# Attention and routing on one core: routing in the next slot, and weights split while the first batch runs

## The chip, the cores and the metric

The kernel runs on one core of one Trainium2 chip. The metric is the device time of a run in microseconds. The profile is of one execution, and its time is given beside that of the timed runs below.

## What is computed

64 batches of 128 tokens of width 512, all fp32. Each batch attends to its own context of 128 tokens, and then each token goes to two of twelve small experts:

```python
q = rms_norm((layernorm(x) @ Wq) by 16 heads of 128) * q_norm_w
k = rms_norm((ctx @ Wk) by 4 heads) * k_norm_w;  v = ctx @ Wv      # 4 query heads share one k, v
x = x + softmax(q @ k.T / sqrt(128)) @ v @ Wo
h = layernorm(x);  logits = h @ gate_w.T                            # 12 experts, the best 2 of each token
x = x + sum over the 2 of  weight * (silu((h @ w1.T) * (h @ w3.T)) @ w2.T)
# an expert takes at most ceil(8192 * 1.25 / 12) tokens per choice list, in token order
```

## The kernel before

The work has three stages: a load of the weights, a loop over the 64 batches (attention and routing), and the experts (`experts`, which the diff leaves alone). A fp32 product is made of three passes of TensorE over a high and a low part of each factor (`PARTS`: hi hi, hi lo, lo hi). So each operand is split: ScalarE writes the high part as a copy in a shorter format, VectorE (POOL for x and the context) writes the low part as the difference.

**Weights.** 40 lots of 256 KB (4 of Wk, 4 of Wv, 16 of Wq, 16 of Wo) go through six staging buffers. Per lot: SyncE (SP) loads it; ScalarE makes the high part (L927); VectorE makes the low part (L1182). A Wq lot is centred first: TensorE computes the column means (`mean`, L706) and VectorE subtracts them (L1178). All of it stands before the loop in each engine's program, and so do the scaling of the norm weights (`scale_weights`), the split of the gate (`split_gate`), and two fills (`d_sent`): the lists of experts in DRAM and 1.8 MB of x copied behind the output. POOL waits for both fills ahead of its loop.

**The loop.** Every engine runs `body(b)` with the same four slots g = 0 to 3, one for each group of four heads; the order in which calls stand there is the order in which the engine works, in order, and semaphores join the engines. A slot holds steps of several batches at once. With u = 4b + g:

- PE: scores of u (L760); half of the keys or values of batch b+1, and queries of u+3 (L716); out projection of u-2 (L787); attend of u-1 (L775). In slot 1 also `route(b-2)` (L796, L797), which writes the logits into OT_B, attend's bank; in slot 3 `positions(b-2)`.
- The probabilities: VectorE takes the maxima (L1031) and nmax (L1034); ScalarE the exponentials (L890) from PSUM; VectorE the reciprocal (L1040) and the normalisation (L1043); ScalarE the high part (L898); VectorE the low part (`split_p`, L1049). SP then turns both (a DMA transpose, `turn_p`), and in the next slot ScalarE (`widen_p`, L904) and VectorE (L1056) bring them to fp32 for attend. In ScalarE's program `widen_p` of u-1 stands ahead of the exponentials of u.
- Between these stand the other steps: the query split (L880, L1022); the key norm (`norm_k`, L997) and key split (`split_k`, L865 and L1003), then `turn_k`, for which the scores of slot 0 wait; `residual` (L1065), `stats_2` (L1069), `norm2` (L1078) of batch b-1; `copy_logits` (L1088), `choose` (L1094 to L1103), `place` of the routing; `split_xn2` and `turn_xn2`, for which `route` waits.

VectorE's order in slots 2 and 3 before, from its `body`:

```python
# slot 1, end: ..., split_p, split_q, sum_k(b+1), choose(b-2)
# slot 2: residual(b-1), maxima, split_o, widen_p, norm_k(b+1), normalise, sum_q, split_p, split_q, stats_2(b-1), split_k(b+1)
# slot 3: maxima, split_o, widen_p, norm2(b-1), normalise, count(b-2), sum_q, split_p, split_q
```

`kn`, into which `norm_k` writes, is the buffer from which `route` reads the turned x, so `norm_k` waits for `lg_done`. The body runs as straight code for b = -1 to 2 and 62 to 66 and as a hardware loop between.

Of the kernel before, what the change touches and what calls it, by code (L numbers as in the profile page):

```python
# [399 lines left out]
def build(nc, x, xT, cT, wq, wk, wv, wo, qw, kw, gateT, w13, w2T, out):  # L400
# [42 lines left out]
    with keep:  # L443
# [13 lines left out]
        with ExitStack() as ctx:  # L457
# [4 lines left out]
            wqp = [sb(f"wq_{p}", [128, NC, NH * HD], f32r) for p in ("hi", "lo")]  # L462
            wkvp = [sb(f"wkv_{p}", [128, 2, NC, NG * HD], f32r) for p in ("hi", "lo")]
            wop = [sb(f"wo_{p}", [128, NH, HID], f32r) for p in ("hi", "lo")]
# [52 lines left out]
            def heads(bank):  # L517
                return bank[:, :].rearrange("p (h t) -> p h t", h=HPG)

            STAGES = (0, 1, 5, 9, 10, 11)  # L520
            NST = len(STAGES)
            d_w = [sem(f"d_w_stage{i}") for i in range(NST)]
            d_small, d_c, d_x, d_xs, d_xr = sem("d_small"), sem("d_c"), sem("d_x"), sem("d_xs"), sem("d_xr")
# [30 lines left out]
            LOTS = ([("k", n) for n in range(NG)] + [("v", n) for n in range(NG)] + [("q", n) for n in range(NH)]  # L554
                    + [("o", n) for n in range(NH)])
            NLOT = len(LOTS)
            V_IN, Q_IN = 2 * NG, 2 * NG

            def stage(l):
                flat = work[:, STAGES[l % NST], :]  # L560
                return flat if LOTS[l][0] == "o" else flat.rearrange("p (c n) -> p c n", c=NC)

            def lot_parts(l):

                kind, n = LOTS[l]
                cols = slice(n * 128, (n + 1) * 128)
                if kind in "kv":
                    return [w[:, "kv".index(kind), :, cols] for w in wkvp]
                if kind == "q":
                    return [w[:, :, cols] for w in wqp]  # L570
                return [w[:, n, :] for w in wop]

            def lot_landed(eng, l):
                eng.wait_ge(d_w[l % NST], 16 * (l // NST + 1))

            def mean_cols(n):

                return (S_B, OT_B, WO_B, SQ_B)[n % 4][:, 0:128]
# [12 lines left out]
            def _(sp):  # L591
# [50 lines left out]
                for l, (kind, n) in enumerate(LOTS):  # L642
                    if l == NG:
                        load_c(0)
                    if l == V_IN:
                        sp.dma_start(gate[:, :, :], gateT).then_inc(d_small, 16)
                        sp.dma_start(wb[:, :], qw.broadcast_to([128, HD])).then_inc(d_small, 16)
                        sp.dma_start(work[:, 6, 0:HD], kw.broadcast_to([128, HD])).then_inc(d_small, 16)
                        load_x(0)
                    if l == Q_IN + NG:  # L650
                        load_stat(0)
                    if l >= NST:
                        sp.wait_ge(w_lo, l - NST + 1)
                    cols = slice(n * 128, (n + 1) * 128)
                    src = (wo[cols, :] if kind == "o" else wq_v[:, :, cols] if kind == "q"
                           else wkv_v["kv".index(kind)][:, :, cols])
                    sp.dma_start(stage(l), src).then_inc(d_w[l % NST], 16)
                sp.wait_ge(s_const, 1)
                sp.dma_start(table_d[LIST1:, :].rearrange("(e p t) o -> p e (t o)", p=128, t=NT),
                             sentinel[:, :, :].rearrange("p t o -> p (t o)")[:, None, :].broadcast_to(  # L660
                                 [128, E, 2 * NT])).then_inc(d_sent, 16)


                sp.dma_start(out[T:T + CP, :], x.rearrange("b t n -> (b t) n")[0:CP, :]).then_inc(d_sent, 16)
                sp.wait_ge(w_lo, NLOT)
                sp.wait_ge(wqk_done, 1)

                def body(b):
                    for g in range(NG):
# [18 lines left out]
                        if g == 0 and live(b - 2):  # L688
                            turn_xn2(b - 2)

# [7 lines left out]
            def _(pe):  # L698

                pe.wait_ge(s_mw, 1)  # L700
                def mean(n):
                    l = Q_IN + n
                    lot_landed(pe, l)
                    wait(pe, w_cent, n - 3)
                    for c in range(NC):
                        mm = nc.tensor.matmul(mean_cols(n), mean_w[:, :], stage(l)[:, c, :],  # L706
                                              start=(c == 0), stop=(c == NC - 1))
                    mm.then_inc(w_mean, 1)
# [11 lines left out]
                def weights_in(b, n):  # L720

                    if isinstance(b, int) and b == 0:
                        pe.wait_ge(w_lo, n)
# [3 lines left out]
                def keys(b, half):  # L727
                    if half == 0:
                        weights_in(b, NG)
                        wait(pe, c_lo, b + 1)  # L730
                        wait(pe, k_nrm, b)
# [4 lines left out]
                def values(b, half):  # L736
                    if half == 0:
                        weights_in(b, V_IN)
                        wait(pe, v_lo, b)
# [4 lines left out]
                def queries(b, g):  # L744
                    u = 4 * b + g
                    weights_in(b, Q_IN + HPG * (g + 1))
# [32 lines left out]
                def out_project(b, g):  # L779
                    u = 4 * b + g  # L780
                    wait(pe, ot_lo, u + 1)
                    if g == 0:
                        wait(pe, x1_done, b)
                    for h in range(HPG):
                        weights_in(b, Q_IN + NH + HPG * g + h + 1)
# [6 lines left out]
                def route(b):  # L792
                    wait(pe, d_xT, 16 * (b + 1))
                    wait(pe, ot_lo, min(4 * b + 8, NU) if isinstance(b, int) else 4 * b + 8)
# [14 lines left out]
                for n in range(NH):  # L809
                    mean(n)  # L810
                pe.wait_ge(s_const, 1)

                def body(b):
                    for g in range(NG):
                        cur, far = (b, g), off(b, g, 3)
                        before, last = off(b, g, -1), off(b, g, -2)
                        if live(b):
                            scores(*cur)
# [6 lines left out]
                        if g == 1 and live(b - 2):  # L825
# [12 lines left out]
            def _(act):  # L838
# [83 lines left out]
                for l, (kind, n) in enumerate(LOTS):  # L922
                    if kind == "q":
                        act.wait_ge(w_cent, n + 1)
                    else:
                        lot_landed(act, l)
                    nc.scalar.copy(lot_parts(l)[0], stage(l)).then_inc(w_hi, 1)  # L927
                    if l == V_IN - 1:
                        split_c(0)
                act.wait_ge(wqk_done, 1)  # L930

                def body(b):
                    for g in range(NG):
                        cur, near, far = (b, g), off(b, g, 2), off(b, g, 3)
                        before, last = off(b, g, -1), off(b, g, -2)
                        if live(last[0]):
# [7 lines left out]
                        if g == 2 and live(b - 2):  # L944
                            exp_diff(b - 2)
# [14 lines left out]
                        if g == 2 and live(b + 1):  # L960
                            split_k(b + 1)
# [5 lines left out]
            def _(dve):  # L967
# [179 lines left out]
                def split_gate():  # L1147

                    for k in range(3):
# [8 lines left out]
                def scale_weights():  # L1158

# [14 lines left out]
                for l in range(NLOT):  # L1174
                    if l + 1 < NLOT and LOTS[l + 1][0] == "q":
                        n, part = LOTS[l + 1][1], stage(l + 1)
                        dve.wait_ge(w_mean, n + 1)
                        nc.vector.tensor_tensor(part, part, mean_cols(n)[:, None, :].broadcast_to([128, NC, 128]),  # L1178
# [192 lines left out]
```

## Time and profile before

| | us |
|---|---|
| timed runs, median (lowest, highest) | 2662.54 (2662.12, 2664.76) |
| the profiled execution | 2652.94 |
| its span | 2651.2 |
| weights before the loop's first step on VectorE | 0 to 55 |
| first and last slot-0 scores (batches 0 and 63) | 79.33 and 2277.68 |
| experts and what comes before them | 2278 to 2651 |

(2277.68 - 79.33) / 63 = 34.89 us for one batch. "Rows" below are lines of the profile: a row of the timeline has start and duration in us, engine, line of the code, operation, output and input, and in brackets how long the engine was idle before it and what ended that. The duration of an instruction includes a tail that overlaps the next: L1003 is 0.66 us long and the next row starts 0.58 us after it. Costs are taken from start to start where both rows are there.

### The profile page before, as it was taken

Reading aid. Unit: us, or ns where it says so; the run is one execution under the profiler, and the core shown is the slowest. Engines: PE = TensorE matmul, PEld = TensorE weight load, DVE = VectorE, ACT = ScalarE, POOL = GpSimd, SP = SyncE. Lnnn points to the kernel's source line nnn. Section 1 sums busy time; section 2 is a strip of 40 time slices with the busy share of each in tenths; the row PEclk is TensorE's granted clock in tenths of the full one; section 3 lists DMA queues with packets and bytes.
Section 4 is the critical chain, followed back from the end, with each engine's and each line's share of the span. In section 5 each row is a group of like instructions: output and inputs, shape, how many; then the busy total and the mean of one; then the engine's idle time right before and its main releaser. Section 6 shows DMA issues by size and latency. Waiting matters only on the chain. (4 is left out here: it accounts for less than half of the span.)

```text
span 2651.2 us, 51686 instructions
## 1 busy us (share of the span) xinstructions
PE 2422.2 (91%) x12985; PEld 1875.8 (71%) x12985; DVE 2082.9 (79%) x5478; ACT 1646.5 (62%) x4789; POOL 1112.9 (42%) x1279
## 2 busy tenths in 40 slices
PE   3899999999999999999999999999999999749883
PEld 3777777777777777777777777777777777525451
DVE  5688888888888888888888888888888878737552
ACT  4566766666666666666666666666666666515441
POOL 0334334343433443434333344344343434258885
PEclk8999999999999999999999999999999999969875
DMA  7455555555555555555555555555555545449997
GB/s 214 84 118 118 122 125 119 125 117 120 127 118 118 116 119 127 119 123 120 118 127 120 120 115 117 126 121 121 123 118 124 123 105 113 97 116 189 182 180 98
DMA packets 778098, 331.20 MB, mean 125 GB/s; under 512 B 695340, under 2 KB 707884, under 8 KB 778032
## 3 DMA queue, kind: packets, MB, share of 16 engines
q1 hardware_dynamic: 754960, 287.61, 48.8%
q0 software_dynamic: 22912, 43.16, 9.1%
q8 instruction: 13, 0.21, 0.0%
q14 instruction: 21, 0.17, 0.0%
q10 hardware_dynamic: 192, 0.04, 0.0%
HBM read 108.15 MB, written 57.71 MB: 63 GB/s over the span
## 5 line engine op out<-in xcount | busy, mean ns | idle before, releaser
L904 ACT CAST pt_hi<-work 128x512 fp32r<-128x512 f16 x256 | 158.9, 621 | 617.9 <-DMA work<-work 617.9
L890 ACT ACTIVATE work<-pb,small 128x128 f32<-128x128 f32 x1024 | 454.5, 454 | 27.4 <-DVE small L1034 27.4
L716 PE MATMUL pb<-wq_hi,x_hi 128*128 128x512 f32 x1024 | 408.8, 399 | 32.2 <-POOL x_lo L1265 22.4
L787 PE MATMUL pb<-wo_hi,ot_hi 128*128 128x512 f32 x1024 | 413.7, 404 | 3.2 <-DVE ot_lo L970 3.0
L716 PE MATMUL pb<-wq_lo,x_hi 128*128 128x512 f32 x1024 | 401.4, 392 | 0.0
L716 PE MATMUL pb<-wq_hi,x_lo 128*128 128x512 f32 x1024 | 401.1, 392 | 0.0
L787 PE MATMUL pb<-wo_lo,ot_hi 128*128 128x512 f32 x1024 | 401.0, 392 | 0.0
L787 PE MATMUL pb<-wo_hi,ot_lo 128*128 128x512 f32 x1024 | 400.4, 391 | 0.0
L1288 POOL TENSOR_TENSOR small<-small 128x4 f32<-128x4 f32 x256 | 155.8, 609 | 544.7 <-DVE small L1016 544.7
L1022 DVE SCALAR_TENSOR_TENSOR work<-pb,small,work 128x128 f16<-128x128 f32 x1024 | 286.7, 340 | 45.1 <-ACT work L880 45.1
L880 ACT ACTIVATE work<-pb,small 128x128 f16<-128x128 f32 x1024 | 291.3, 366 | 0.0
L1291 POOL TENSOR_TENSOR small<-small 128x4 f32<-128x4 f32 x256 | 267.4, 1044 | 29.5 <-POOL small L1288 18.7
L1049 DVE TENSOR_TENSOR work<-work 128x512 f16<-128x512 f32 x256 | 251.3, 982 | 18.1 <-ACT work L898 12.0
L1265 POOL TENSOR_TENSOR x_lo<-work,x_hi 128x512 fp32r<-128x512 f32 x64 | 82.3, 1286 | 424.6 <-ACT x_hi L849 378.4
L716 PEld LDWEIGHTS pb<-wq_hi,x_hi 128*128 128x128 f32 x1024 | 193.6, 189 | 94.0 <-issue 29.0
L787 PEld LDWEIGHTS pb<-wo_hi,ot_hi 128*128 128x128 f32 x1024 | 192.9, 188 | 47.7 <-DVE ot_lo L970 10.7
L716 PEld LDWEIGHTS pb<-wq_hi,x_lo 128*128 128x128 f32 x1024 | 194.0, 189 | 41.4
L716 PE MATMUL pb<-wkv_hi,c_hi 128*128 128x512 f32 x512 | 222.7, 435 | 0.1
L787 PEld LDWEIGHTS pb<-wo_hi,ot_lo 128*128 128x128 f32 x1024 | 193.2, 189 | 41.5
L716 PEld LDWEIGHTS pb<-wq_lo,x_hi 128*128 128x128 f32 x1024 | 194.1, 190 | 39.2
L760 PEld LDWEIGHTS pb<-work 128*128 128x128 f16 x3072 | 172.3, 98 | 68.8 <-issue 68.8
L787 PEld LDWEIGHTS pb<-wo_lo,ot_hi 128*128 128x128 f32 x1024 | 193.6, 189 | 33.9
(144 smaller groups left out, 5297.6 us busy)
## 6 DMA issues: line engine op xcount, KB each, us to landing
work<-x SPq DMA_DIRECT2D x128, 256.0 KB, 3.2
work<-cT SPq DMA_DIRECT2D x64, 256.0 KB, 2.8
work<-xT SPq DMA_DIRECT2D x64, 256.0 KB, 3.2
out<-work SPq DMA_DIRECT2D x64, 256.0 KB, 4.7
xn_scratch<-work SPq DMA_DIRECT2D x64, 256.0 KB, 2.0
work<-work SPq DMA_TRANSPOSE x640, 3.3
work<-wq SPq DMA_DIRECT2D x16, 256.0 KB, 3.1
work<-wo SPq DMA_DIRECT2D x16, 256.0 KB, 3.5
```

What stands on the lines that cost most here:

```text
L716: mm = nc.tensor.matmul(bank[:, :], lhs[a][:, c, :], rhs[b_][:, c, :], start=(c == 0 and n == 0), stop=(c == NC - 1 and n == 2))
L760: mm = nc.tensor.matmul(S_B[:, h * 128:(h + 1) * 128], qT16[:, 4 * a + h, :], kT16[:, 4 * b_ + g, :], start=(n == 0), stop=(n == 2))
L787: mm = nc.tensor.matmul(WO_B[:, :], otp[a][:, h, :], wop[b_][:, g * HPG + h, :], start=(g == 0 and h == 0 and n == 0), stop=(g == NG - 1 a ...
L880: hi = nc.scalar.activation(q16[:, h, :], Q_BS[g % 2][:, h * 128:(h + 1) * 128], ACT.Copy, scale=q_rms[g % 2][:, h:h + 1])
L890: ex = nc.scalar.activation(probs[:, cols], S_B[:, cols], ACT.Exp, bias=nmax[:, h:h + 1], scale=esc, accum_out=psums[:, h:h + 1])
L904: nc.scalar.copy(ptp[0][:, :, :], pT16[:, HI, :]).then_inc(pt_hi, 1)
L1022: lo = nc.vector.scalar_tensor_tensor(out=q16[:, 4 + h, :], in0=Q_BS[g % 2][:, h * 128:(h + 1) * 128], scalar=q_rms[g % 2][:, h:h + 1], in ...
L1049: nc.vector.tensor_tensor(p16[:, LO, :], probs.rearrange("p (h t) -> p h t", h=HPG), p16[:, HI, :], ALU.subtract).then_inc(p_lo, 1)
L1265: nc.gpsimd.tensor_tensor(xp[1][:, :, :], raw_x.rearrange(by_chunk, c=NC), xp[0][:, :, :].bitcast(f32), ALU.subtract).then_inc(x_lo, 1)
L1288: nc.gpsimd.tensor_tensor(q_ms, q_ssq, eps_x.broadcast_to([128, HPG]), ALU.add).then_inc(q_m, 1)
L1291: nc.gpsimd.tensor_tensor(q_rms[g % 2], q_ms, neghalf, ALU.pow).then_inc(q_r, 1)
```

## The change

Two parts. **Routing:** `route` moves from slot 1 to slot 2 on TensorE, `copy_logits` and `choose` with it on VectorE, attend's wait for the copied logits from g = 0 to g = 1. Around it `norm_k` goes from ahead of `normalise` to behind `split_q` in slot 2, `split_k` from the end of slot 2 to slot 3 ahead of the exponentials (ScalarE) and of `norm2` (VectorE), `exp_diff` from slot 2 to the end of slot 3. **Weights:** the raw weights are loaded in ten lots of 1 MB into the space of the low parts, where VectorE replaces them in place; the steps of a lot stand inside `body` at the slots in `FEED`. SP issues the lots of k, q, v; ScalarE those of Wo, in slots 0 and 1 of batch 0. The gate is split in slot 0 of batch 1, the fills are issued in slot 1 of batch 1, and POOL waits for them in batch 2. An instruction still covers 128 x 512 elements: four per lot.

```diff
+            W_SHAPES = (("wq", [128, NC, NH * HD]), ("wkv", [128, 2, NC, NG * HD]), ("wo", [128, NH, HID]))
+            with ExitStack() as before:
+                wq_raw, wkv_raw, wo_raw = (before.enter_context(nc.sbuf_tensor(f"{n}_raw", shape, f32))
+                                           for n, shape in W_SHAPES)
+            wq_lo, wkv_lo, wo_lo = (sb(f"{n}_lo", shape, f32r) for n, shape in W_SHAPES)
...
+            LOTS = [("k", 0), ("q", 0), ("v", 0), ("q", 1), ("q", 2), ("q", 3)] + [("o", n) for n in range(NG)]
+            FEED = {(-1, 0): (0,), (-1, 1): (1,), (-1, 2): (2, 3), (-1, 3): (4,), (0, 0): (5,),
+                    (0, 2): (6,), (0, 3): (7,), (1, 0): (8,), (1, 1): (9,)}
...
@@ sync
+                load_c(0)
+                load_lot(0)
+                load_x(0)
...
+                for l in range(1, 6):
+                    load_lot(l)
...
+                        if g == 1 and isinstance(b, int) and b == 1:
+                            fill_tables()
@@ tensor
+                def mean(l):
+                    n = LOTS[l][1]
+                    pe.wait_ge(d_w[l], 16)
+                    wait(pe, w_cent, NC * (n - 1))
                     for c in range(NC):
+                        mm = nc.tensor.matmul(mean_bank(n)[:, :], mean_w[:, :], raw(l)[:, c, :],
                                               start=(c == 0), stop=(c == NC - 1))
...
@@ attend
                     if g == 0:
                         wait(pe, v_lo, b + 1)
+                    if g == 1:
                         wait(pe, lg_cp, b - 1)
@@ tensor, body
+                        for l in lots(b, g):
+                            if LOTS[l][0] == "q":
+                                mean(l)
                         if live(b):
                             scores(*cur)
...
-                        if g == 1 and live(b - 2):
+                        if g == 2 and live(b - 2):
                             route(b - 2)
@@ scalar
+                def head_of_lot(l):
+                    kind, n = LOTS[l]
+                    if kind != "q":
+                        act.wait_ge(d_w[l], 16)
+                    for c in range(NC):
+                        if kind == "q":
+                            act.wait_ge(w_cent, NC * n + c + 1)
+                        nc.scalar.copy(lot_parts(l)[0][:, c, :], raw(l)[:, c, :]).then_inc(w_hi, 1)
...
+                        for l in lots(b, g):
+                            head_of_lot(l)
+                        if g < 2 and isinstance(b, int) and b == 0:
+                            load_wo(6 + 2 * g)
+                            load_wo(7 + 2 * g)
...
-                        if g == 2 and live(b - 2):
-                            exp_diff(b - 2)
+                        if g == 3 and live(b + 1):
+                            split_k(b + 1)
                         if live(b):
                             exps(*cur)
...
-                        if g == 2 and live(b + 1):
-                            split_k(b + 1)
+                        if g == 3 and live(b - 2):
+                            exp_diff(b - 2)
@@ vector
+                def rest_of_lot(l):
+                    kind, n = LOTS[l]
+                    hi, lo = lot_parts(l)
+                    if kind == "q":
                         dve.wait_ge(w_mean, n + 1)
+                        for c in range(NC):
+                            nc.vector.tensor_tensor(raw(l)[:, c, :], raw(l)[:, c, :], mean_bank(n)[:, :],
+                                                    ALU.subtract).then_inc(w_cent, 1)
+                    for c in range(NC):
+                        dve.wait_ge(w_hi, NC * l + c + 1)
+                        nc.vector.tensor_tensor(lo[:, c, :], raw(l)[:, c, :], hi[:, c, :].bitcast(f32),
+                                                ALU.subtract).then_inc(w_lo, 1)
...
+                        if g == 1 and isinstance(b, int) and b == -1:
+                            scale_weights()
+                            dve.wait_ge(wqk_done, 6)
+                        for l in lots(b, g):
+                            rest_of_lot(l)
+                        if g == 0 and isinstance(b, int) and b == 1:
+                            split_gate()
...
-                        if g == 2 and live(b + 1):
-                            norm_k(b + 1)
+                        if g == 3 and live(b + 1):
+                            split_k(b + 1)
                         if g == 3 and live(b - 1):
                             norm2(b - 1)
                         if live(b):
                             normalise(*cur)
-                        if g == 1 and live(b - 2):
+                        if g == 2 and live(b - 2):
                             copy_logits(b - 2)
...
+                        if g == 2 and live(b + 1):
+                            norm_k(b + 1)
-                        if g == 1 and live(b - 2):
+                        if g == 2 and live(b - 2):
                             choose(b - 2)
                         if g == 2 and live(b - 1):
                             stats_2(b - 1)
-                        if g == 2 and live(b + 1):
-                            split_k(b + 1)
@@ gpsimd
-                pool.wait_ge(d_sent, 32)
...
+                        if g == 1 and isinstance(b, int) and b == 2:
+                            pool.wait_ge(d_sent, 32)
```

## Rows read from the trace of the kernel before

**Rows 1.** Waits, 400 to 1900 us, 43 batches: who waited for whom, total us, times, longest.
```profile
ACT pt_hi L904 <- DMA work<-work: 415.3, 172, 3.1
...
DVE small L1040 <- ACT work L890: 101.5, 129, 1.1
...
PE pb L796 <- DMA work<-work: 41.0, 43, 1.1
```

**Rows 2.** The page: engines, and DMA issues with KB each and us to landing.
```profile
PE 2422.2 (91%) x12985; PEld 1875.8 (71%) x12985; DVE 2082.9 (79%) x5478; ACT 1646.5 (62%) x4789; POOL 1112.9 (42%) x1279
...
work<-work SPq DMA_TRANSPOSE x640, 3.3
```

**Rows 3.** Timeline, VectorE, L1049 of batch 0 and of one steady batch: start us, us.
```profile
87.90 1.35 DVE L1049 TENSOR_TENSOR work<-work 128x512 f16<-128x512 f32 x1 [0.35 <-ACT work L898]
...
97.08 0.69 DVE L1049 TENSOR_TENSOR work<-work 128x512 f16<-128x512 f32 x1
...
105.13 0.69 DVE L1049 TENSOR_TENSOR work<-work 128x512 f16<-128x512 f32 x1
...
1018.08 1.31 DVE L1049 TENSOR_TENSOR work<-work 128x512 f16<-128x512 f32 x1
...
1027.16 1.23 DVE L1049 TENSOR_TENSOR work<-work 128x512 f16<-128x512 f32 x1 [0.16 <-ACT work L898]
...
1036.14 0.69 DVE L1049 TENSOR_TENSOR work<-work 128x512 f16<-128x512 f32 x1
...
1044.84 0.69 DVE L1049 TENSOR_TENSOR work<-work 128x512 f16<-128x512 f32 x1
...
1052.92 1.31 DVE L1049 TENSOR_TENSOR work<-work 128x512 f16<-128x512 f32 x1
```

**Rows 4.** Timeline, VectorE, end of slot 1 to slot 3 of the steady batch.
```profile
1038.83 0.16 DVE L1094 MAX8 small<-small 128x8 f32<-128x12 f32 x1
...
1039.67 0.68 DVE L1065 TENSOR_TENSOR work<-work,pb 128x512 f32<-128x512 f32 x1
...
1040.99 0.23 DVE L1034 TENSOR_SCALAR small<-small 128x4 f32<-128x4 f32 x1
...
1042.22 1.13 DVE L997 SCALAR_TENSOR_TENSOR work<-pb,small,wqk_rows 128x128 f32<-128x128 f32 x4
...
1046.93 0.68 DVE L1069 BATCH_NORM_STATS2 small<-work 128x6 f32<-128x512 f32 x1
...
1047.80 0.66 DVE L1003 TENSOR_TENSOR work<-work 128x512 f16<-128x512 f32 x1
1048.38 0.69 DVE L1031 TENSOR_REDUCE small<-pb 128x4 f32<-128x512 f32 x1
...
1051.33 0.18 DVE L1040 RECIPROCAL small<-small 128x4 f32<-128x4 f32 x1 [0.62 <-ACT work L890]
```

**Rows 5.** Timeline, ScalarE, slots 2 and 3 of the steady batch.
```profile
1040.10 0.62 ACT L904 CAST pt_hi<-work 128x512 fp32r<-128x512 f16 x1 [1.94 <-DMA work<-work]
...
1041.26 0.46 ACT L890 ACTIVATE work<-pb,small 128x128 f32<-128x128 f32 x1 [0.43 <-DVE small L1034]
...
1045.73 0.64 ACT L865 CAST work<-work 128x512 f16<-128x512 f32 x1
...
1048.90 0.62 ACT L904 CAST pt_hi<-work 128x512 fp32r<-128x512 f16 x1 [2.05 <-DMA work<-work]
1049.43 0.46 ACT L890 ACTIVATE work<-pb,small 128x128 f32<-128x128 f32 x1
```

**Rows 6.** Groups by line, 0 to 60 us: xcount, busy us, mean ns, idle before.
```profile
L706 PE MATMUL pb<-work,mean_w 128*128 128x128 f32 x128 | 18.3, 299 | 18.8 <-DMA work<-wq 18.7
...
L1182 DVE TENSOR_TENSOR wq_lo<-work,wq_hi 128x512 fp32r<-128x512 f32 x16 | 11.0, 685 | 0.1
```

**Rows 7.** Busy time by stretch: us, busy and count of each engine, clock, DMA share, GB/s.
```profile
0.00:33.00 33.00, 15.46 (x107) 14.07 (x108) 19.32 (x36) 13.79 (x22) 2.86 (x14) 1.00 0.74 210
```

**Rows 8.** DMA issues of the whole span: xcount, KB each, median us to landing.
```profile
out<-x SPq DMA_DIRECT2D x1, 1792.0 KB, 11.7
```

More of the change, by code:

```diff
@@ L518, in heads @@
                 return bank[:, :].rearrange("p (h t) -> p h t", h=HPG)
[L520 to L523, printed above, removed]
+            d_w = [sem(f"d_w_lot{i}") for i in range(2 + 2 * NG)]
+            d_small, d_gate, d_c, d_x, d_xs, d_xr = sem("d_small"), sem("d_gate"), sem("d_c"), sem("d_x"), sem("d_xs"), sem("d_xr")
             d_x1, d_xn2, d_sent = sem("d_x1_stored"), sem("d_xn2_stored"), sem("d_sentinel")
@@ L551, in build, with lots, lot_of, raw @@
             block = ctx.enter_context(nc.Block())
[L554 to L561, printed above, removed]
-            def lot_parts(l):
[L565 to L578, printed above, removed]
+            LOTS = [("k", 0), ("q", 0), ("v", 0), ("q", 1), ("q", 2), ("q", 3)] + [("o", n) for n in range(NG)]
+            FEED = {(-1, 0): (0,), (-1, 1): (1,), (-1, 2): (2, 3), (-1, 3): (4,), (0, 0): (5,),
+                    (0, 2): (6,), (0, 3): (7,), (1, 0): (8,), (1, 1): (9,)}
+            def lots(b, g):
+                return FEED.get((b, g), ()) if isinstance(b, int) else ()
+            def lot_of(l, wq_, wkv_, wo_):
+                kind, n = LOTS[l]
+                if kind in "kv":
+                    return wkv_[:, "kv".index(kind), :, :]
+                if kind == "q":
+                    return wq_[:, :, n * 512:(n + 1) * 512]
+                return wo_[:, n * HPG:(n + 1) * HPG, :]
+            def lot_parts(l):
+                return lot_of(l, wq_hi, wkv_hi, wo_hi), lot_of(l, wq_lo, wkv_lo, wo_lo)
+            def raw(l):
+                return lot_of(l, wq_raw, wkv_raw, wo_raw)
+            def mean_bank(n):
+                return (OT_B, WO_B)[n % 2]
+            def chunks_done(kind, n=0):
+                return NC * (LOTS.index((kind, n)) + 1)
             def loop(eng, body):
@@ new lines, in fill_tables @@
+                def fill_tables():
+                    sp.dma_start(table_d[LIST1:, :].rearrange("(e p t) o -> p e (t o)", p=128, t=NT),
+                                 sentinel[:, :, :].rearrange("p t o -> p (t o)")[:, None, :].broadcast_to(
+                                     [128, E, 2 * NT])).then_inc(d_sent, 16)
+                    sp.dma_start(out[T:T + CP, :],
+                                 x.rearrange("b t n -> (b t) n")[0:CP, :]).then_inc(d_sent, 16)
+                load_c(0)
@@ L793, in route @@
                     wait(pe, d_xT, 16 * (b + 1))
-                    wait(pe, ot_lo, min(4 * b + 8, NU) if isinstance(b, int) else 4 * b + 8)
+                    wait(pe, ot_lo, min(4 * b + 9, NU) if isinstance(b, int) else 4 * b + 9)
                     for c in range(NC):
```

84 lines of the change are left out of this document (26 added, 58 removed).

## Prediction

> **What bounds the kernel now.** I read the page first: TensorE is busy 91% of the span, more than any other engine [rows 2]. Then the waits of 43 steady batches [rows 1]. TensorE has one row there: `route` (L796) waits for a transposed tile, 41.0 us in 43 times, 0.95 us a batch. That looks like the bound and its one gap. But the same table has no row in which VectorE or SP waits for TensorE. ScalarE waits for the turned probabilities in every slot (415.3 us, 172 times = 4 x 43) and VectorE waits for ScalarE's exponentials (101.5 us). So there is a second loop, beside TensorE: `split_p` (L1049), DMA, `widen_p` (L904), exponentials (L890), reciprocal (L1040), normalise, `split_p` of the next slot.
>
> Third view: the timeline of one steady batch. The five starts of L1049 [rows 3] give the four slots: 9.08 (into slot 0), 8.98 (slot 1), 8.70 (slot 2), 8.08 (slot 3), sum 34.84 us, which is the pitch of the whole loop, (2277.68 - 79.33)/63 = 34.89. Slot 3 is to be followed link by link: L1049 at 1044.84; L904 at 1048.90, 4.06 later, as soon as the DMA lands; first exponential 0.53 later, 1049.43; L1040 at 1051.33, 1.90 later, freed by the exponentials (0.62 idle before it); L1049 1.59 later, 1052.92 [rows 3 to 5]. There is no slack in it. This loop, through ScalarE, VectorE and the DMA, makes the pitch; TensorE runs ahead of it and takes its spare time at `route`, whose tile is turned behind `turn_p` on the same queue.
>
> **Routing, slot 2.** `choose` leaves the end of slot 1: 0.84 us from L1094 to L1065 [rows 4]. Now the exponentials start at 1041.26 after 0.43 us of waiting for nmax [rows 5]; nmax is done at 1040.99 + 0.23 = 1041.22 [rows 4], so then at 40.38. ScalarE is ready at 1040.10 + 0.53 = 40.63, `exp_diff` being gone from that place. They start at 40.63. `norm_k` no longer stands before the reciprocal, so the two links of slot 3 follow: 40.63 + 1.90 + 1.59 = 44.12 instead of 44.84: **-0.72**. A control for this: batch 0 had no `choose` and no `exp_diff`, and its slot 2 took 105.13 - 97.08 = 8.05 [rows 3], against 8.70, a saving of 0.65. `copy_logits` ahead of `split_p` waits for `route`; TensorE is done with it before (its queries of that slot are needed by ScalarE's square, right behind the exponentials), and the 0.1 us reduction fits beside ScalarE's L898: 0, at worst 0.2.
>
> **Routing, slot 3.** Count from L1049 of slot 2. `split_q` ends at 46.93 - 44.84 = 2.09 (start of L1069). Before: `stats_2` 0.87, `split_k` 0.58, then maxima at 3.54 [rows 4], and nmax came just in time for ScalarE. After: `norm_k` 1.05 (1.13 less the 0.08 that overlaps), `choose` 0.84, `stats_2` 0.87, maxima at 4.85. From maxima to exponentials: 41.26 - (39.67 + 0.60 of the residual) = 0.99. So the exponentials start at 5.84; ScalarE's own path, 4.06 + 0.53 + 0.53 for `split_k` that now stands there (L865), would allow 5.12 [rows 5] and is hidden under it. Reciprocal at 7.74: VectorE, with `split_k` now between, is free at 4.85 + (51.33 - 48.38 - 0.62) + 0.58 = 7.76, the same. L1049 at 7.76 + 1.59 = 9.35 instead of 8.08: **+1.27**. The bounds: if the two delays didn't add and only the reordered `split_k` counted, +0.53 (ScalarE alone); if the transposes crowd each other, +1.6: `turn_k` is now issued some 2 us ahead of `turn_p`, and a transpose takes 3.3 us to land [rows 2], so up to 0.3 may be added.
>
> **Routing, slots 0 and 1, and TensorE.** ScalarE's and VectorE's orders are as before, so 9.08 and 8.98 stay. `turn_k` goes out behind `split_k` at 4.85 + 0.99 - 0.1 + 0.9 (the output and probability splits) + 0.58 = 7.2 to 7.8, lands at about 11, and slot 0's scores can start then; they take under 1 us. Maxima of slot 0 stand at 9.35 + 1.31 + 1.1 = 11.8 and nmax is wanted only 4.06 + 0.5 + 0.5 after L1049: hidden by 2 us. TensorE has 33.9 us of work a batch in 34.84 and the stall at `route` goes; it waits elsewhere (the key tile, the output split), and frees nobody. **The sum of the loop is -0.72 + 1.27 = +0.55 us a batch**, times 62 batches with routing: +34 us; bounds +0.3 to +0.9 a batch, +19 to +56.
>
> **Weights.** I follow the chain to `split_p` of slot 0, batch 0, which stood at 87.90 [rows 3]. A centring pass or low part takes 0.60 start to start (0.685 long [rows 6]), so a q lot costs VectorE 8 x 0.60 = 4.8 us, others 2.4. The mean of a whole q lot is 4 times the columns of an old one: at most 18.3/4 = 4.6 us [rows 6], less if weight loads carried part of it; I take 3.5. DMA moved 210 GB/s in the first 33 us [rows 7]: the context, k, x, small ones and q0 are 3.0 MB, 14.3 us, landed at 15. Then in series, because queries(0,g) waits for its lot, the mean of the next lot stands behind them on TensorE, and VectorE waits for that mean: mean 18.5; q0 split 23.5; queries 27.5 (slow clock); mean q1 31; v and q1 split 36; queries 39; mean q2 42.5; split 47.3; queries 50.3; mean q3 53.8 (scores of slot 0 behind it); split 58.6; queries(0,3) 61.5; square, sum, `split_p` 64. That is 24 us earlier than 87.90; VectorE's work alone (44 passes of 0.60 and the rest) sets a floor near 45, a slower clock and 4.6 us means put it at 70: gain 18 to 40.
>
> What it gives back inside batches 0 and 1: four Wo lots, 2.4 us each on VectorE ahead of the maxima; batch 0's slots have some 0.9 to 1.9 us of slack there, so 1.5, 1.9, 0.5, 1.3. ScalarE's heads lie in its wait for the DMA. `split_gate` 1.1. 4 MB of Wo move on another queue beside the transposes (20 us at 210 GB/s): 3 us of later landings. The fill, 11.7 us alone [rows 8], stands in SP's queue ahead of slot 2's `turn_p`, which comes 8.7 us later: 3 us, at most 11.7. Together 12 (5 to 25). The net of the start is 24 - 12: **-12 us** (+5 to -30). The experts and the drain are untouched.
>
> On whose share of DMA time the 3 us hang: the Trainium skill, page "DMA: Bandwidth & Descriptors", section "Queues, rings and completion order", has each DMA engine take turns by packet between the rows of queues that have work. No row of the kernel before shows ScalarE loads beside transposes; by that rule alone a transpose of 3.3 us beside them would double, 3.3 us for each of the two or three slots, and the sum would be 4 to 7 us higher.
>
> **Sum.** 2652.94 (span and 1.7 us around it) + 34 - 12 = 2675. The timed median stands 9.6 us above the profiled execution; the difference carries over: 2662.5 + 22 = **2684.5**.
>
> **Rivals.**
> - *A: TensorE is the bound.* The stall at `route` goes and nothing replaces it: 62 x 0.95 = -59, start -12: 2591. For it: 91% busy, one gap with one cause. Against: nobody waits for TensorE, and the loop of the probabilities has no idle link. It would also need that loop to lose over 1 us a batch where the edits add to it. Chance 0.07. [...]
> - *B: slot 3 costs no more than slot 2 saves.* With the lower bound, +0.53 - 0.72, or both parts of `choose` and `norm_k` finding gaps: loop 0 to -0.2, start -12: 2645 to 2650. Against: rows 4 are back to back. Chance 0.17.
> - *C: the key tile decides (slower side).* `turn_k` lands at 11; if scores of slot 0 come over 2 us later than I have it, maxima, nmax and exponentials wait for TensorE, and each us beyond is paid 62 times: at 1 us more, 2684.5 + 62 = 2746. Chance 0.10.
> - *D: the loop as forecast, but the start gains 30 net*: 2666. Inside my range. Chance 0.08; the forecast itself 0.58.
>
> The forecast's own range is 2660 to 2707. The range of 8 in 10 takes B in and leaves A and C out: 2646 to 2712. A measurement here tells about 0.2% (5.3 us) from no change. Faster by more: A, nearly all of B, a little of the forecast: 0.26. Within: 0.12. Slower: 0.62.
>
> **What would show it.** In the new trace: slots of L1049 of about 9.1, 9.0, 8.0, 9.35; first exponential of slot 3 released by nmax, not by ScalarE's order; no TensorE wait at L796's successor, but one of about 1 us at the scores of slot 0 for the key tile, and short ones at the out projection for `ot_lo`; pitch 35.4; `split_p` of batch 0, slot 0, near 64. I am wrong if slot 3 stays under 8.7, or if the pitch falls towards 33.9.

## The result and the profile after

The changed kernel takes 2702.45 us in the median of 4 runs (2701.61 to 2703.17), the kernel before 2662.33: ratio 1.0151, 95% interval 1.0133 to 1.0168, 40.1 us slower. The forecast was 2684.5, 22 us slower.

The view that decides is the timeline of VectorE over one steady batch, as in [rows 3, 4]: start us, us, engine, line. Line numbers have moved: L1077 is `split_p` (L1049 before), L1025 `norm_k` (L997), L1122 `choose` (L1094), L1097 `stats_2` (L1069), L1059 the maxima (L1031), L1068 the reciprocal (L1040).

```profile
1498.85 1.31 DVE L1077 TENSOR_TENSOR work<-work 128x512 f16<-128x512 f32 x1
...
1507.96 1.24 DVE L1077 TENSOR_TENSOR work<-work 128x512 f16<-128x512 f32 x1 [0.16 <-ACT work L912]
...
1517.03 0.69 DVE L1077 TENSOR_TENSOR work<-work 128x512 f16<-128x512 f32 x1
...
1525.06 0.69 DVE L1077 TENSOR_TENSOR work<-work 128x512 f16<-128x512 f32 x1
...
1527.14 1.12 DVE L1025 SCALAR_TENSOR_TENSOR work<-pb,small,wqk_rows 128x128 f32<-128x128 f32 x4
1528.18 0.17 DVE L1122 MAX8 small<-small 128x8 f32<-128x12 f32 x1
...
1529.03 0.69 DVE L1097 BATCH_NORM_STATS2 small<-work 128x6 f32<-128x512 f32 x1
...
1529.90 0.69 DVE L1059 TENSOR_REDUCE small<-pb 128x4 f32<-128x512 f32 x1
...
1532.80 0.18 DVE L1068 RECIPROCAL small<-small 128x4 f32<-128x4 f32 x1
...
1534.39 1.32 DVE L1077 TENSOR_TENSOR work<-work 128x512 f16<-128x512 f32 x1
```

The starts of L1077 give the slots: 1498.85 to 1507.96 (slot 0, 9.11), to 1517.03 (slot 1, 9.07), to 1525.06 (slot 2, 8.03), to 1534.39 (slot 3, 9.33), together 35.54 where the kernel before had 34.84 [rows 3]. In slot 3 `norm_k`, `choose`, `stats_2` and the maxima follow each other with no gap: `norm_k` at 2.08 after L1077, `choose` at 3.12, `stats_2` at 3.97, maxima at 4.84, reciprocal at 7.74, L1077 at 9.33. ScalarE in slots 2 and 3 shows the same from its side (L918 is `widen_p`, L879 `split_k`, L904 the exponentials):

```profile
1521.02 0.62 ACT L918 CAST pt_hi<-work 128x512 fp32r<-128x512 f16 x1 [1.98 <-DMA work<-work]
1521.56 0.46 ACT L904 ACTIVATE work<-pb,small 128x128 f32<-128x128 f32 x1
...
1529.17 0.62 ACT L918 CAST pt_hi<-work 128x512 fp32r<-128x512 f16 x1 [2.44 <-DMA work<-work]
1529.70 0.61 ACT L879 CAST work<-work 128x512 f16<-128x512 f32 x1
1530.89 0.46 ACT L904 ACTIVATE work<-pb,small 128x128 f32<-128x128 f32 x1 [0.58 <-DVE small L1062]
```

In slot 2 the exponentials follow `widen_p` at once; the 0.43 us of waiting of [rows 5] is gone. In slot 3 they now wait 0.58 us for nmax; `split_k`, which stands ahead of them, is done before that and costs nothing here. The waits from 400 to 1900 us, 42 batches (who waited for whom, total, times, longest):

```profile
ACT pt_hi L918 <- DMA work<-work: 435.5, 169, 3.1
...
ACT work L904 <- DVE small L1062: 29.7, 42, 1.0
...
PE pb L818 <- DVE ot_lo L998: 22.9, 42, 0.7
PE pb L800 <- DVE ot_lo L998: 20.8, 42, 0.5
...
PE pb L772 <- DMA work<-work: 13.5, 42, 0.4
```

TensorE no longer waits at `route`. It waits at `positions` (L818) and the out projection (L800) for the output split and at the scores (L772) for the key tile, 57.2 us in 42 batches, 1.36 us each, against 0.95 us before [rows 1]. So it got 0.4 us more of waiting where a wait was taken from it.

Means of the slots, worked out from the starts of `split_p` in 12 batches of each trace up to 700 us:

| kernel | slot 0 | 1 | 2 | 3 | pitch |
|---|---|---|---|---|---|
| before | 9.07 | 9.02 | 8.71 | 8.04 | 34.84 |
| after | 9.11 | 9.04 | 8.05 | 9.33 | 35.53 |

**The start.** `split_p` of batch 0, slot 0, is at 69.72 us instead of 87.90 [rows 3]: 18.2 us earlier. At slot 0 of batch 2 it stands at 157.89 instead of 156.10: all given back, and 1.8 more. One trace fixes such a difference only to a us or two: in the seven traces with the old load of the weights the first `split_p` comes at 86.39 to 88.66, and in the five of them whose batches 0 and 1 run as before that of slot (2,0) comes at 154.48 to 156.10. The slots of batches 0 and 1 one by one, from (0,1) to (2,0): 14.84, 9.57, 10.01, 10.17, 10.00, 7.99, 14.73, 10.86, where the kernel before has 9.18, 8.05, 8.05, 8.65, 9.08, 8.03, 8.02, 9.14. Two are long. ScalarE's row in slot (0,1), with its DMA issues (ACTq):

```profile
62.59 1.03 ACTq L949 DMA_DIRECT2D wo_raw<-wo  x2
...
68.87 0.37 ACTq L949 DMA_DIRECT2D wo_raw<-wo  x1
...
80.07 0.62 ACT L918 CAST pt_hi<-work 128x512 fp32r<-128x512 f16 x1 [9.33 <-DMA work<-work]
```

The transpose that SP issued at 71.15 releases `widen_p` at 80.07, 8.9 us later (the median on the page of this profile is 3.2), while the four Wo lots of 1 MB that ScalarE issued from 62.59 to 69.28 are landing. That issue and those of slot (1,3) on SP, then ScalarE in slot (1,3):

```profile
71.15 1.24 SPq L640 DMA_TRANSPOSE work<-work  x1
...
126.98 0.77 SPq L663 DMA_DIRECT2D out<-x  x1
127.86 1.53 SPq L635 DMA_TRANSPOSE work<-work  x1
```

```profile
138.40 1.14 ACT L894 ACTIVATE work<-pb,small 128x128 f16<-128x128 f32 x4 [6.14 <-DMA work<-work]
...
139.88 0.65 ACT L918 CAST pt_hi<-work 128x512 fp32r<-128x512 f16 x1
```

L663 is the fill of the output, 1.8 MB. Right behind it on SP stands `turn_q` (L635), issued at 127.86; it releases ScalarE's split of the queries (L894) at 138.40, 10.5 us later, after 6.14 us idle. `widen_p` and VectorE's `split_q` stand behind that.

**The account.** The last `split_p` is 41.1 us later than before (2351.32, 2310.24), the first step of the experts (`first_n`) 39.0 later. The rest of the span, unchanged code, took 319.3 us in the profiled execution and 308.0 in that of before; in the other profiles it is 315 to 320 on the chip where the kernel before took 2660.9 (315.2 with the loop of the kernel before, in e8 below) and 309 to 312 elsewhere (312.4 with the changed loop, in e2). So 11.3 of the 50.3 us between the two spans go with the execution, not with the change. The timed medians, 40.1 apart, agree with the 39.0.

### The profile page after: what moved, and what is told of

Same layout as the page of the kernel before. It is cut to its first block and busy times, and to the rows that moved or that the text cites. A ratio compares the mean times of both kernels' runs of the same rounds, so it can differ in the third digit from the quotient of the medians.

```text
span 2701.5 us, 51516 instructions
## 1 busy us (share of the span) xinstructions
PE 2455.9 (91%) x12889; PEld 1878.1 (70%) x12889; DVE 2079.6 (77%) x5478; ACT 1646.6 (61%) x4789; POOL 1107.4 (41%) x1279
## 5 line engine op out<-in xcount | busy, mean ns | idle before, releaser
L918 ACT CAST pt_hi<-work 128x512 fp32r<-128x512 f16 x256 | 159.0, 621 | 655.7 <-DMA work<-work 655.7
L904 ACT ACTIVATE work<-pb,small 128x128 f32<-128x128 f32 x1024 | 454.5, 454 | 51.1 <-DVE small L1062 51.1
L800 PE MATMUL pb<-wo_hi,ot_hi 128*128 128x512 f32 x1024 | 420.1, 410 | 41.2 <-DVE ot_lo L998 41.2
L728 PE MATMUL pb<-wq_hi,x_hi 128*128 128x512 f32 x1024 | 403.2, 394 | 18.9 <-DVE wq_lo L1216 13.6
L800 PE MATMUL pb<-wo_lo,ot_hi 128*128 128x512 f32 x1024 | 401.5, 392 | 0.0
L800 PE MATMUL pb<-wo_hi,ot_lo 128*128 128x512 f32 x1024 | 401.3, 392 | 0.0
L1326 POOL TENSOR_TENSOR small<-small 128x4 f32<-128x4 f32 x256 | 171.0, 668 | 530.5 <-DVE small L1044 530.5
L1050 DVE SCALAR_TENSOR_TENSOR work<-pb,small,work 128x128 f16<-128x128 f32 x1024 | 286.8, 341 | 53.4 <-ACT work L894 53.4
L894 ACT ACTIVATE work<-pb,small 128x128 f16<-128x128 f32 x1024 | 291.3, 366 | 6.5 <-DMA work<-work 6.5
L1329 POOL TENSOR_TENSOR small<-small 128x4 f32<-128x4 f32 x256 | 258.7, 1011 | 29.5 <-POOL small L1326 18.7
L800 PEld LDWEIGHTS pb<-wo_hi,ot_hi 128*128 128x128 f32 x1024 | 193.0, 189 | 103.5 <-DVE ot_lo L998 69.3
L1077 DVE TENSOR_TENSOR work<-work 128x512 f16<-128x512 f32 x256 | 250.6, 979 | 17.7 <-ACT work L912 11.7
L772 PEld LDWEIGHTS pb<-work 128*128 128x128 f16 x3072 | 173.4, 98 | 102.4 <-issue 53.2
L772 PE MATMUL pb<-work 128*128 128x128 f16 x3072 | 217.2, 221 | 25.0 <-DMA work<-work 24.0
L800 PEld LDWEIGHTS pb<-wo_hi,ot_lo 128*128 128x128 f32 x1024 | 193.4, 189 | 42.8
```

Source lines behind the costliest of these rows:

```text
L728: mm = nc.tensor.matmul(bank[:, :], lhs[a][:, c, :], rhs[b_][:, c, :], start=(c == 0 and n == 0), stop=(c == NC - 1 and n == 2))
L772: mm = nc.tensor.matmul(S_B[:, h * 128:(h + 1) * 128], qT16[:, 4 * a + h, :], kT16[:, 4 * b_ + g, :], start=(n == 0), stop=(n == 2))
L800: mm = nc.tensor.matmul(WO_B[:, :], otp[a][:, h, :], wop[b_][:, g * HPG + h, :], start=(g == 0 and h == 0 and n == 0), stop=(g == NG - 1 a ...
L894: hi = nc.scalar.activation(q16[:, h, :], Q_BS[g % 2][:, h * 128:(h + 1) * 128], ACT.Copy, scale=q_rms[g % 2][:, h:h + 1])
L904: ex = nc.scalar.activation(probs[:, cols], S_B[:, cols], ACT.Exp, bias=nmax[:, h:h + 1], scale=esc, accum_out=psums[:, h:h + 1])
L918: nc.scalar.copy(ptp[0][:, :, :], pT16[:, HI, :]).then_inc(pt_hi, 1)
```

## Experiments

Each was timed beside the kernel before on the same chip; its median there was 2652.3 for e1, e2, e3 and e7, 2660.9 for e4, e5, e6 and e8, and 2656.0 for e9 to e12. Slots and pitches come from the timelines as above.

**Half and half.** `e1_weights_only`: the changed kernel with every line of the routing part as before. `e2_routing_only`: the kernel before with those lines of the change.

```diff
# in words. e1: after, minus; e2: before, plus:
 g == 2: route, copy_logits, choose;  norm_k behind split_q;  split_k and exp_diff in slot 3
```

> The changed kernel with its routing put back where it was; only the new load of the weights is left. Theory (the loop of the probabilities sets the pitch, and the start gives back what it gained): pitch 34.83 as before, slots 9.07, 9.02, 8.71, 8.03; split_p of batch 0, slot 0, near 69.7 us as in the changed kernel, but by slot 0 of batch 2 nothing of the 18 us is left; time 2662 +- 4. Rival (the weights part costs in every batch, by memory or queue contention): pitch above 35 and a time above 2680.

Measured: ratio 1.0015 (1.0005 to 1.0025), +4 us; slots 9.10, 9.03, 8.71, 8.03, pitch 34.87; `split_p` at 70.16, that of slot (2,0) at 157.07. As the theory had it: no cost by the batch, and a start that ends 1 us behind, in a trace that is good to a us or two.

> The kernel before with the routing part alone. Theory: slots 9.10, 9.04, 8.04, 9.33, pitch 35.52, +0.69 us a batch, 62 times = +43 us: 2703 +- 4. Rival (TensorE is the bound and its new waits for the key tile or the output split come from the late weights): near 2662 or less.

Measured: ratio 1.0140 (1.0123 to 1.0157), +37 us; slots 9.07, 9.04, 8.04, 9.34, pitch 35.49. The slots came as expected, the time 6 us under the 43: the 0.65 us a batch holds, and a single stall of 4 us that the kernel before has and this order hides takes off most of the rest (below). The loss is the routing part's.

**Is TensorE the bound?** `e8_less_pe`:

```diff
-                        for n, (a, b_) in enumerate(PARTS):
+                        for n, (a, b_) in enumerate(PARTS[:2]):      # out_project
```

> The kernel before without the third pass (low part of the output times high part of Wo) of the out projection: 16 of TensorE's matmuls of 128x512 less in each batch, 3.6 us of its 33.9. It leaves out that part of the product. Theory (TensorE does not set the pitch): pitch 34.83, time within 4 us of 2662, and TensorE waits 3.6 us more a batch. Rival A (TensorE is the bound): up to -3.6 x 62 = -225 us.

Measured: ratio 0.9994 (0.9984 to 1.0004), pitch 34.81. TensorE's waits in 43 batches, and its busy time from 1000 to 1300 us (us, TensorE, its loads, VectorE, ...) in e8 and in the kernel before:

```profile
PE pb L716 <- DVE work L1022: 70.8, 87, 1.4
PE pb L796 <- DMA work<-work: 41.7, 43, 1.1
PE pb L787 <- DVE ot_lo L970: 17.1, 43, 0.4
PE pb L775 <- DVE small L1112: 10.0, 43, 0.4
```

```profile
1000.00:1300.00 300.00, 273.34 (x1505) 204.49 (x1503) 253.91 (x707) 200.16 (x609) 120.73 (x149) 1.00 0.54 120
...
1000.00:1300.00 300.00, 292.63 (x1642) 232.61 (x1641) 254.81 (x709) 201.96 (x611) 121.32 (x149) 1.00 0.55 121
```

TensorE's busy time is 273.3 us of 300 where the kernel before has 292.6, which is 2.2 us less a batch; the 16 matmuls a batch are gone (1505 records for 1642), but the busy time fell by less than the 3.6 expected. It came back as waits: 70.8 us at the queries for `q_lo`, 41.7 at `route`, 17.1 and 10.0 elsewhere, 3.25 us a batch against 0.95. Were TensorE the bound, 2.2 x 63 would have made -139 us. The engine with the highest busy share does not set the pitch. One row of the kernel before does have an engine waiting for TensorE, ScalarE for attend, 0.2 us a batch. In e8 that row is gone and the time stays, so the wait is off the path:

```profile
ACT ot_hi L910 <- PE pb L775: 9.2, 41, 0.3
```

**What in slot 3?** `e4_norm_k_early`, the routing part with `norm_k` back ahead of `normalise`:

> Routing part alone, but norm_k back ahead of normalise in slot 2; choose stays at the end of slot 2. Theory: VectorE's maxima of slot 3 come 1.05 us earlier, and then ScalarE's split_k in front of the exponentials binds: slot 3 = 5.12 + 1.90 + 1.59 = 8.6; slot 2 = 8.0 to 8.3, since norm_k must wait for route. Pitch 34.8 to 35.1 and a time of 2662 to 2679. If the order on VectorE were not the cause of slot 3's 9.33, it stays at 9.3 and the time at 2703.

```diff
+                        if g == 2 and live(b + 1):
+                            norm_k(b + 1)          # ahead of split_k / norm2 / normalise again
```

Measured: 1.0118 (1.0101 to 1.0135), +31 us; slot 3 is 8.52, slot 2 is 8.71, pitch 35.31. Slot 3 followed the order on VectorE (8.6 forecast), but slot 2 lost the whole gain, not 0.3 of it, and the pitch lies above the 35.1 expected. That was the first sign that something else holds slot 2. Its trace names it, POOL and not `route`:

```profile
1232.43 1.13 DVE L998 SCALAR_TENSOR_TENSOR work<-pb,small,wqk_rows 128x128 f32<-128x128 f32 x4 [0.93 <-POOL small L1281]
```

**Can slot 2's gain be had alone?** `e3_choose_slot3`:

```diff
-                        if g == 1 and live(b - 2):
+                        if g == 3 and live(b - 2):
                             choose(b - 2)           # VectorE, end of the slot
-                        if g == 3 and live(b - 2):
-                            count(b - 2)
+                        if g == 0 and live(b - 3):
+                            count(b - 3)            # positions(b - 3) on TensorE likewise
```

> The kernel before with choose (0.84 us of VectorE) moved from the end of slot 1, where the maxima of slot 2 wait behind it, to the end of slot 3, where the maxima of slot 0 have 2 us of slack before the exponentials; positions and count follow into slot 0 of the next body, exp_diff to the end of slot 3. Route stays in slot 1 with its stall. Theory: slot 2 falls from 8.71 to 8.04, the others stay, pitch 34.16, -0.67 x 62 = -41: 2621 +- 5, and TensorE's stall at route shrinks by the same 0.67 a batch. Rival A (TensorE is the bound through its stall at route): the time stays within 5 us of 2662.

Measured: 1.0002 (0.9993 to 1.0012), slot 2 at 8.71, pitch 34.78. The expectation failed by all of it, and rival A's number came out, though not for rival A's reason (e8). VectorE in slot 2, then POOL just before:

```profile
1520.89 0.69 DVE L1050 TENSOR_TENSOR work<-work 128x512 f16<-128x512 f32 x1
...
1524.17 0.69 DVE L1032 TENSOR_REDUCE small<-pb 128x4 f32<-128x512 f32 x1
...
1526.98 1.13 DVE L998 SCALAR_TENSOR_TENSOR work<-pb,small,wqk_rows 128x128 f32<-128x128 f32 x4 [0.93 <-POOL small L1281]
...
1529.60 0.73 DVE L1050 TENSOR_TENSOR work<-work 128x512 f16<-128x512 f32 x1
```

```profile
1522.99 1.11 POOL L1304 DMA_INDIRECT token_table<-small  x1 [0.19 <-issue]
1524.40 0.99 POOL L1304 DMA_INDIRECT token_table<-small  x1 [0.30 <-issue]
1525.46 0.20 POOL L1278 TENSOR_SCALAR small<-small 128x4 f32<-128x4 f32 x1
1525.74 1.20 POOL L1281 TENSOR_TENSOR small<-small 128x4 f32<-128x4 f32 x1
```

The maxima did come early: 1524.17 is 3.28 after L1050. In the kernel before they start 0.61 behind the residual's 1039.67 [rows 4], at 1040.28, 4.14 after L1049. But now `norm_k` (L998) waits 0.93 us for POOL, whose program has `scatter(b-3)`, two indirect DMAs, 2.4 us, ahead of the key's root (L1278, L1281). The row was in the trace of the kernel before, on POOL:

```profile
1038.25 1.11 POOL L1303 DMA_INDIRECT token_table<-small  x1 [0.18 <-issue]
...
1041.00 1.19 POOL L1280 TENSOR_TENSOR small<-small 128x4 f32<-128x4 f32 x1
```

Its key root ends at 1042.19 and `norm_k` starts at 1042.22 [rows 4]. Two limits of nearly the same length lay side by side, and I had read one.

**Both limits.** `e9_choose_and_scatter` is e3 with POOL's order turned; `e10_scatter_only` is that turn alone.

```diff
-                        if g == 1 and live(b - 3):
-                            scatter(b - 3)
                         if g == 1 and live(b + 1):
                             rms_k(b + 1)
+                        if g == 1 and live(b - 3):
+                            scatter(b - 3)
```

> e3_choose_slot3 showed slot 2 at 8.71 still, with norm_k waiting 0.93 us for POOL, whose scatter of batch b-3 (two indirect DMAs, 2.4 us) stands ahead of rms_k in slot 1. Here the choose move of e3 and, on POOL, rms_k ahead of scatter. New theory (slot 2 has two limits side by side, VectorE's choose and POOL's scatter, and either alone gives 8.71): slot 2 falls to 8.04, pitch 34.1, 0.7 x 61 = 43 us faster than the kernel before. If a third limit stands there too, or TensorE's 33.9 us of work binds first, less: down to 0.

> The kernel before with the POOL order alone (rms_k ahead of scatter). New theory: choose still stands ahead of the maxima of slot 2 and norm_k ahead of the reciprocal; VectorE's row is full there, so slot 2 stays within 0.15 of 8.71 and the time within 8 us. If POOL alone was the limit: slot 2 at 8.04 and -43 us.

Measured: e9 0.9846 (0.9829 to 0.9863), -43 us; slots 9.09, 9.02, 8.01, 8.04, pitch 34.15. One batch of e9 on VectorE:

```profile
1000.69 1.32 DVE L1050 TENSOR_TENSOR work<-work 128x512 f16<-128x512 f32 x1
...
1009.76 1.24 DVE L1050 TENSOR_TENSOR work<-work 128x512 f16<-128x512 f32 x1
...
1018.79 0.69 DVE L1050 TENSOR_TENSOR work<-work 128x512 f16<-128x512 f32 x1
...
1023.86 1.12 DVE L998 SCALAR_TENSOR_TENSOR work<-pb,small,wqk_rows 128x128 f32<-128x128 f32 x4
...
1026.78 0.69 DVE L1050 TENSOR_TENSOR work<-work 128x512 f16<-128x512 f32 x1
...
1034.82 1.32 DVE L1050 TENSOR_TENSOR work<-work 128x512 f16<-128x512 f32 x1
```

The starts of L1050 are 9.07, 9.03, 7.99 and 8.04 apart, and `norm_k` (L998) comes 5.07 after L1050 instead of 6.09 in e3. e10: 0.9967 (0.9956 to 0.9978); slot 2 8.64, as expected, pitch 34.73: POOL's limit was the longer of the two, by 0.07. The time, -9.6 us, is a little more than the 8 allowed. Of it some 7 follow from the pitch and 4 from a stall that the 12 batches of the table leave out. In batch 59 of the kernel before POOL's second indirect DMA stands 4.47 us behind the first instead of 0.30, `norm_k` waits for it, and slot 2 is 12.72 us long:

```profile
2158.46 1.00 POOL L1303 DMA_INDIRECT token_table<-small  x1 [4.47 <-issue]
...
2160.88 1.13 DVE L997 SCALAR_TENSOR_TENSOR work<-pb,small,wqk_rows 128x128 f32<-128x128 f32 x4 [4.09 <-POOL small L1280]
```

With `scatter` behind `rms_k` (e9, e10, e11) or with `norm_k` behind `split_q` (e2, the changed kernel) POOL stalls at the same place, for 3.18 to 4.75 us, and slot 2 of batch 59 is no longer than the others.

**The start.** `e5_wo_early` and `e6_fill_early` are the changed kernel with one thing each issued by SP behind the last Wq lot; `e7_best` has both, with the loop of e3.

```diff
                 for l in range(1, 6):
                     load_lot(l)
+                for l in range(6, 10): ...          # e5: Wo by SP, not by ScalarE in batch 0
                 sp.wait_ge(s_const, 1)
+                fill_tables()                        # e6: not in slot 1 of batch 1
```

> The changed kernel with the four Wo lots issued by SP behind the Wq lots instead of by ScalarE in batch 0. Theory: the transpose of slot 0, batch 0, which landed 9 us after its issue, lands in 4; slot (0,1) falls from 14.84 to about 9.2: 2702.5 - 5.7 = 2697. If slot (0,1) was long for another reason: 2702.

> The changed kernel with the two fills issued behind the Wq lots instead of in slot 1 of batch 1. Theory: slots (1,3) and (2,0) fall from 14.73 and 10.86 to 9.3 and 9.1: -7 us, 2695. If slot (1,3) is long for another reason: 2702.

> The loop of e3_choose_slot3 with the new load of the weights, but the four Wo lots and the two fills issued by SP right behind the Wq lots, where the DMA has nothing to do for 40 us. Theory: pitch 34.16 (-41 us); the start keeps 18.2 us less the 5.9 us that the four Wo lots cost VectorE in batches 0 and 1 (-12 us): 2609 +- 6. If Wo loads and fill were not what lengthened slots (0,1) and (1,3), the start gives nothing: 2621.

Measured: e5 1.0139 (1.0122 to 1.0156), +37 us; slot (0,1) is 9.21 instead of 14.84. e6 1.0130 (1.0113 to 1.0147), +34 us; slot (1,3) is 8.67 instead of 14.73, but (2,0) stays at 10.98. Their intervals overlap that of the changed kernel, so the slots are the evidence here, not the times. By slot 0 of batch 2 they are 4.3 and 5.3 us ahead of the changed kernel, less than the slots gave, since in e5 the fill's slot grew to 15.70 and in e6 `split_p` started 3 us later, of which 2.4 came back in slot (0,1), 12.49. e7 0.9968 (0.9955 to 0.9980), -9 us: slot (0,1) 9.19, (1,3) 8.06, pitch 34.87 as e3's loop gives none, and the start worth 10.4 us at slot (2,0). The start is near the 12 expected, the loop is the failed one of e3, and the time is far from the 2609 expected.

**The version that beats both.** `e12_start_only` also moves the low parts of three Wo lots to VectorE's idle times before batch 0; `e11_best` is that start with the loop of e9.

```diff
+            LOTS = [("k", 0), ("q", 0), ("v", 0), ("q", 1), ("o", 0), ("q", 2), ("o", 1), ("o", 2), ("q", 3), ("o", 3)]
+            FEED = {(-1, 0): (0,), (-1, 1): (1,), (-1, 2): (2, 3, 4), (-1, 3): (5, 6, 7), (0, 0): (8,), (1, 0): (9,)}
```

> The start of e11 with the loop of the kernel before. -16 us against it, pitch 34.85; e7_best, with Wo's low parts in batches 0 and 1, gave -8.7. If the low parts of Wo delay q lots or queries before batch 0, split_p of batch 0 comes after 72 and the gain is below 12.

> The loop of e9, with the new load of the weights changed in three places: all ten lots and the two fills issued by SP at once; the low parts of Wo in VectorE's idle times before batch 0 (slots 2 and 3 of body -1) and in slot 0 of batch 1, where nmax has 2 us of slack. Start: split_p of batch 0 at 70 as in the changed kernel, and batches 0 and 1 as long as before, but for the 1.8 us of slot (2,0) that all kernels with the new load show: -16 us; with the loop, -59 us against the kernel before. If e9's loop gives nothing: -16.

Measured: e12 0.9957 (0.9941 to 0.9974), -13 us; slot (2,0) stands at 138.54, 17.6 us earlier than before, and 4 are lost later to a pitch of 34.91. e11 0.9799 (0.9783 to 0.9815), 2601.3 us against 2656.0: -55 us, 4 short of the 59 expected; pitch 34.21.

## Why the prediction was right, by its steps

- *The loop of the probabilities sets the pitch.* Held: e8 took 2.2 us of TensorE's busy time out of each batch and the time stayed. Rival A is out. That nobody waits for TensorE was not quite so: ScalarE does, 9.2 us in 43 batches.
- *Slot 2, -0.72.* Measured -0.66. The step was right for the change, which took `norm_k` out of the way; but it named only VectorE's `choose` and was blind to POOL's `scatter`, as e3 and e4 showed. My control, slot 2 of batch 0 at 8.05, had neither a `choose` nor a `scatter` and so could not tell them apart.
- *Slot 3, +1.27.* Measured +1.29, link by link as written (maxima 4.85 and 4.84, reciprocal 7.76 and 7.74, end 9.35 and 9.33).
- *Slots 0 and 1, nothing.* +0.04 and +0.02. The key tile is late, as said, and costs TensorE 0.3 us a batch (13.5 us in 42, the waits above), where I had written about 1, and nobody else: rival C is out.
- *The sum of the loop, +34 us.* 39.3 from slot (2,0) to the last `split_p` (2193.4 us, 2154.1 before), and e2 alone 37. The term was low by the small ones: 0.06 a batch in slot 2, 0.06 in slots 0 and 1, 0.02 in slot 3, together 0.69 instead of 0.55, which times 62 would be 43. That it came out nearer, at 39.3, is luck: the 4 us stall of batch 59, which I had not seen, is in slot 2 of the kernel before and not in the path of the changed one.
- *Start, 24 us earlier.* 18.2; `split_p` came at 69.7, not 64. The means took 4.8, 4.0, 3.6 and 3.7 us against 3.5, some 2 us more in all. Three blocks of queries took 5.3, 4.4 and 4.4 us, 14.1 where the chain had 10, since their matmuls started 0.43 us apart for most of it, at a granted clock of 0.50 (the 1.2 GHz level); I had put that clock into the first block alone, and no row of mine showed it. The window of the first block (us, TensorE, its loads, VectorE, ScalarE, POOL, then PEclk, DMA share, GB/s):

```profile
24.60:28.40 3.80, 3.80 (x10) 2.97 (x9) 0.00 (x0) 0.00 (x0) 0.00 (x0) 0.50 0.20 74
```

  From 39.5 to 42.8 and from 53.4 to 56.3 us the clock reads 0.50 too. TensorE had stood idle for 3.66, 3.14 and 3.90 us ahead of the three blocks; the fourth came after 2.87 us of idling, ran at 1.00 with matmuls 0.23 us apart, and took 2.9. And the v lot's 2.4 us on VectorE, read as hidden, held the centring of the second Wq lot up by some 1.3: its mean ends near 32.4, and the first subtraction starts at 33.73. The k and first Wq lots, on the other hand, were there 1.6 us early, 13.4 for 15.
- *Given back inside batches 0 and 1, 12 us.* This is the term that was mis-sized most: 20. Wo beside the transposes 5.7 in slot (0,1) instead of 3, as e5 shows; the fill 6.1 instead of 3 in slot (1,3) (14.73, and 8.67 in e6), by way of `turn_q` and not of slot 2's `turn_p`, and 0.65 there by the new order; the four lots and the split of the gate 5.9 in the slots (0,2) to (1,1), where I had 5.2 and 1.1 for them; and 1.7 us in slot (2,0), which every kernel with the new load has and none without: a transpose issued at 136.14 in e7 landed 5.05 us later. What delays it stays open. One difference is on record and was not tested: in the 6 us behind `split_p` of slot (1,3) a load of instructions crosses the DMA in all seven traces with the new load and in none of the seven without it. In e7 (packets, MB, share of 16 engines, from 136 to 142 us):

```profile
q8 instruction: 1, 0.02, 1.0%
```

- *The net of the start, -12.* +1.8, and up to 3.4 against the other traces with the old load. Rivals B and D rested on it and on a free slot 3, and are out.

So sign and mechanism were right, and 18 us were missing (40.1 less 22): up to the last `split_p` the trace has +1.8 for -12 and +39.3 for +34, 19 us together; the drain gave 2 back, and 1 is between the trace and the medians.

## What to carry to other kernels

An engine that is busy 91% and shows one wait need not be the bound: look whether anybody waits for it and whether that wait is on the path, and follow the loop that nobody waits inside of, link by link, through every engine it crosses, in-order programs included. Before moving work out of a full row, look for a second wait that ends at the same time on another engine, for only both together may give the gain (e3 nothing, e10 0.3%, e9 1.5%). Loads that feed a later stage belong where the DMA is idle, not beside the transposes on which the loop hangs.

## What the runs showed of the hardware

- A DMA transpose that takes 3.2 us in the median took 8.9 while 4 MB issued by another engine were landing, and 10.5 behind a 1.8 MB copy in its own queue. By the Trainium skill, page "DMA: Bandwidth & Descriptors", section "Queues, rings and completion order", two queues with work take turns by packet; the doubling to 6.6 us, the prediction's estimate from that, is less than the 8.9 seen. No run here shows in what turns the packets went.
- The changed kernel's lots of 1 MB move at 378 to 389 GB/s between 12 and 25 us, where the first 33 us of the kernel before have 210 in the mean [rows 7]. Whether the size of the lots, the six staging buffers or the small loads among them make the difference was not tested. The changed kernel's start in stretches (us, busy of TensorE, its loads, VectorE, ScalarE, POOL, then PEclk, DMA share, GB/s):

```profile
12.00:20.00 8.00, 7.25 (x17) 3.40 (x15) 2.52 (x7) 1.05 (x2) 0.00 (x0) 1.00 1.05 389
20.00:25.00 5.00, 1.82 (x4) 1.49 (x5) 3.12 (x6) 1.37 (x3) 0.00 (x0) 0.74 1.05 378
```

- POOL issues 128 indirect DMAs, two a batch, and stands idle 0.30 us between the two of a pair. Ahead of the 114th it stands 3.18 to 5.39 us, in all 14 traces and there alone. Why at the 114th, no run here shows. What it costs hangs on what stands behind it in POOL's program: 4 us of slot 2 with `rms_k` behind it and `norm_k` early (the kernel before), under 1 us of slot 3 with `rms_k` ahead of it (e9, e10, e11).
- The same code of the experts' stage took from 308 to 320 us from one execution to another, more than most effects here. A difference of a few us between two spans is to be read in the stage that changed.
